# Filler matmuls on TensorE before the first tile, and an earlier copy of tile 0's first half, in a two-layer graph network kernel

## What is computed

```python
h = jnp.maximum(_layernorm(x, axis=-1), 0.0)
x = x + _L0_gnn_ref(h, edge_index, edge_type_2, ...)
h = jnp.maximum(_layernorm(x, axis=-1), 0.0)
x = x + _L1_gnn_ref(h, L1_gnn_W, L1_gnn_a, src, dst)
```

## Time and profile before

| What | us |
|---|---|
| median of 3 runs | 508.41 (508.1 to 508.73) |
| the profiled execution | 509.32 |
| its span, first to last instruction | 507.5 |
| mean granted TensorE clock | 0.998 |

### The profile page before, as it was taken

The page is one execution under the profiler, slowest core; times in us unless marked ns, Lnnn a source line. Parts: engine busy times, 40 slices in busy tenths (PEclk is TensorE's granted clock), DMA queues, the critical chain, the costliest instruction groups (busy, mean ns, idle before and its releaser), DMA issues.

```text
span 507.5 us, 7735 instructions
## 1 busy us (share of the span) xinstructions
PE 491.8 (97%) x2953; PEld 424.1 (84%) x2953; DVE 372.1 (73%) x636; ACT 227.5 (45%) x383; POOL 79.5 (16%) x81
## 2 busy tenths in 40 slices
PE   2999999999999999999999999999999999999996
PEld 2989998989989999898888888888887878777785
DVE  4845886599999999998955555556598877777634
ACT  5765543424866666669722223334133323323211
POOL 1181323200000000002000000000083333322400
PEclk9999999999999999999999999999999999999999
DMA  8972254413013335237921111000032322222211
GB/s 256 232 241 88 81 170 142 128 37 95 22 42 94 102 95 159 82 120 260 329 71 42 40 44 50 29 1 0 1 81 83 93 90 65 77 82 81 82 43 45
DMA packets 22186, 49.15 MB, mean 97 GB/s; under 512 B 4798, under 2 KB 10709, under 8 KB 22018
## 3 DMA queue, kind: packets, MB, share of 16 engines
q1 hardware_dynamic: 20879, 44.66, 29.3%
q0 software_dynamic: 1264, 3.93, 2.2%
HBM read 33.05 MB, written 16.85 MB: 98 GB/s over the span
## 4 chain that ended last, share of the span: by engine, by line
PE 90%; DVE 5%; ACT 3%; DMA 1%; issue 1%; SPq 0%; DVEq 0%; ACTq 0%
PE ps L1359 11%; PE ps L1628 9%; PE ps L1630 9%; PE ps L1629 9%; PE ps L1525 8%; PE ps L1610 7%; PE ps L1611 7%; PE ps L1609 7%; PE ps L1428 4%; PE ps L1447 2%; PE ps L1581 2%; PE ps L1595 2%; PE ps L1583 2%; PE ps L1582 2%; PE ps L1403 1%; PE ps L1406 1%
## 5 line engine op out<-in xcount | busy, mean ns | idle before, releaser
L1628 PE MATMUL ps<-h_hi,att_hi 125*125 125x512 f32 (+1 forms) x190 | 73.5, 387 | 0.0
L1629 PE MATMUL ps<-h_lo,att_hi 125*125 125x512 f32 (+1 forms) x190 | 72.6, 382 | 0.0
L1630 PE MATMUL ps<-h_hi,att_lo 125*125 125x512 f32 (+1 forms) x190 | 72.6, 382 | 0.0
L1609 PE MATMUL ps<-wg,gT_hi 128*125 128x512 f32 x160 | 63.7, 398 | 0.0
L1610 PE MATMUL ps<-wg,gT_hi 128*125 128x512 f32 x160 | 63.1, 394 | 0.0
L1611 PE MATMUL ps<-wg,gT_lo 128*125 128x512 f32 x160 | 63.0, 394 | 0.0
L1525 PE MATMUL ps<-msg_hi,adj_hi 125*125 125x288 f32 x180 | 50.3, 304 | 0.0
L1525 PE MATMUL ps<-msg_lo,adj_hi 125*125 125x286 f32 x180 | 45.9, 295 | 0.0
L708 ACT ACTIVATE em<-ps,rinv 125x512 f32<-125x512 f32 (+1 forms) x21 | 14.0, 669 | 63.1 <-DVE hp L1225 63.1
L1630 PEld LDWEIGHTS ps<-h_hi,att_lo 125*125 125x125 f32 x190 | 35.3, 186 | 8.0
L1628 PEld LDWEIGHTS ps<-h_hi,att_hi 125*125 125x125 f32 x190 | 35.2, 185 | 7.9
(11 more groups left out here) (218 smaller groups left out, 1085.8 us busy)
## 6 DMA issues: line engine op xcount, KB each, us to landing
xt<-in_x SPq DMA_DIRECT2D x10, 448.0 KB
xh_scratch<-xt SPq DMA_DIRECT2D x10, 448.0 KB
xt<-xh_scratch SPq DMA_DIRECT2D x10, 448.0 KB
x_scratch<-xt SPq DMA_DIRECT2D x10, 448.0 KB
x1t<-x_scratch SPq DMA_DIRECT2D x10, 448.0 KB
xr<-x_scratch SPq DMA_DIRECT2D x10, 448.0 KB
out_x<-xr SPq DMA_DIRECT2D x19, 224.0 KB
wg_raw<-in_L_gnn_W POOLq DMA_DIRECT2D x7, 512.0 KB, 7.5
```

The lines of the kernel that those rows point to most:

```text
L1609: M.matmul(to, hi, wg[k][:, 0, cut], start=n == 0, stop=False)
L1628: M.matmul(to, hi[:, s, :], h_hi[:, s, cut], start=s == 0, stop=False)
L1629: M.matmul(to, hi[:, s, :], h_lo[:, s, cut], start=False, stop=False)
L1630: return M.matmul(to, lo[:, s, :], h_hi[:, s, cut], start=False, stop=s == TILES - 1)
```

## The change

Four things. VectorE, after its increments and before its first wait, fills the second half of `junk` with ones and signals `filled`. TensorE, after its own increments, waits for `filled`, multiplies that half with itself ten times (125 rows, 125 columns of weights, 512 columns moved, bf16, into bank 7), then waits for the layer-norm weights as before and transposes them, and multiplies six times more. ScalarE's `first_transposed` and VectorE's `first_low_parts` are each cut in two calls: the first half is done after `norm(0)` on ScalarE, ahead of `deviation(1)`, and after `variance(1)` on VectorE, ahead of `deviation(1)`; the second half keeps its place. The semaphore `msgpad`, which one instruction incremented and none waited for, is gone.

```diff
--- before.py
+++ after.py
@@ -253,7 +253,7 @@
 
         names = """edges_in lnw_in lnw_ps w_split h1_rdy bias_in g_ps wo_split xh_rdy x1_rdy o_ps wg_rdy a_in gT_ps h_dve
             res_rdy zeros consts more_consts sd_rdy ssq_rdy rm_rdy hT_hi_rdy g_act win_out c_used e_rdy yT_hi_rdy
-            g1_rdy gT_hi_rdy h_act att_e att_hi_rdy m_rdy asum_rdy sum_step el_rdy r_ps msgpad var_rdy rstd_rdy hT_ps wraw_hi rms_rdy
+            g1_rdy gT_hi_rdy h_act att_e att_hi_rdy m_rdy asum_rdy sum_step el_rdy r_ps filled var_rdy rstd_rdy hT_ps wraw_hi rms_rdy
             table_rdy x_used hot_used s_ps c_ps wo_hi_rdy yT_ps rs2_rdy sd2_rdy wg_hi_rdy rstd2_rdy h_ps
             al_ps al_rdy att_v att_p p_ps rinv_rdy bn_rdy rs_rdy hT_lo_rdy g_dve win_lo deg_rdy inv_rdy
             z1_rdy zz_rdy y_rdy yT_lo_rdy bn2_rdy mv2_rdy gT_lo_rdy att_u att_lo_rdy den_rdy rr_rdy dchain
@@ -541,10 +541,10 @@
                     last = A.copy(hT_hi[b][:, 4 * h:4 * h + 4, :], first_tp(t, h))
                 last.then_inc(S["hT_hi_rdy"], 1)
 
-            def first_transposed():
-                for h, (came_in, out) in enumerate((("half_hT", "half_hi"), ("hT_ps", "hT_hi_rdy"))):
-                    act.wait_ge(S[came_in], data(0) if h else 1)
-                    A.copy(hT_hi[0][:, 4 * h:4 * h + 4, :], tp_bank(h)).then_inc(S[out], 1)
+            def first_transposed(h):
+                came_in, out = (("half_hT", "half_hi"), ("hT_ps", "hT_hi_rdy"))[h]
+                act.wait_ge(S[came_in], data(0) if h else 1)
+                A.copy(hT_hi[0][:, 4 * h:4 * h + 4, :], tp_bank(h)).then_inc(S[out], 1)
 
             def split_weights(ks):
                 for k in ks:
@@ -560,14 +560,15 @@
             def pads():
                 A.copy(ident_r[:], ident[:])
                 A.copy(msg_hi[:, :, :, F], ones[:].rearrange("p (t r) -> p t r", r=RELS))
-                A.mul(msg_hi[:, :, :, F + 1], ones[:].rearrange("p (t r) -> p t r", r=RELS), 0.0).then_inc(S["msgpad"], 1)
+                A.mul(msg_hi[:, :, :, F + 1], ones[:].rearrange("p (t r) -> p t r", r=RELS), 0.0)
 
             act.wait_ge(S["lnw_ps"], 2)
             deviation(0, 0)
             norm(0, 0)
+            first_transposed(0)
             deviation(1, 1)
             split_weights(range(0, 1))
-            first_transposed()
+            first_transposed(1)
             norm(1, 1)
             split_weights(range(1, 2))
             transposed(1, 1, 0)
@@ -937,11 +938,11 @@
                                            hT_hi[b][:, 4 * h:4 * h + 4, :].bitcast(F32), ALU.subtract)
                 last.then_inc(S["hT_lo_rdy"], 1)
 
-            def first_low_parts():
-                for h, (came_in, out) in enumerate((("half_hi", "half_lo"), ("hT_hi_rdy", "hT_lo_rdy"))):
-                    dve.wait_ge(S[came_in], data(0) if h else 1)
-                    V.tensor_tensor(hT_lo[0][:, 4 * h:4 * h + 4, :], tp_bank(h), hT_hi[0][:, 4 * h:4 * h + 4, :].bitcast(F32),
-                                    ALU.subtract).then_inc(S[out], 1)
+            def first_low_parts(h):
+                came_in, out = (("half_hi", "half_lo"), ("hT_hi_rdy", "hT_lo_rdy"))[h]
+                dve.wait_ge(S[came_in], data(0) if h else 1)
+                V.tensor_tensor(hT_lo[0][:, 4 * h:4 * h + 4, :], tp_bank(h), hT_hi[0][:, 4 * h:4 * h + 4, :].bitcast(F32),
+                                ALU.subtract).then_inc(S[out], 1)
 
             def mean_square(t):
                 dve.wait_ge(S["rm_rdy"], data(t))
@@ -990,12 +991,14 @@
             def stage1(first, end):
                 pipeline((transposed, 1), (messages, 2), (moments, -1), steps=(first, end))
 
+            V.memset(junk[:, HALF:D], 1.0).then_inc(S["filled"], 1)
             dve.wait_ge(S["consts"], 1)
             moments(0, 0, 0)
             variance(1, 1)
+            first_low_parts(0)
             deviation(1, 1)
             split_weights(range(0, 1))
-            first_low_parts()
+            first_low_parts(1)
             split_weights(range(1, 2))
             low_parts(1, 1)
             split_weights(range(2, KT))
@@ -1348,9 +1351,15 @@
                 pe.sem_inc(S[n], CREDIT)
             pe.sem_inc(S["p_ps"], 2 * CREDIT)
             pe.sem_inc(S["c_ps"], 3 * CREDIT)
+            def kept_busy(times):
+                for _ in range(times):
+                    M.matmul(bank(7, T, HALF), junk[0:T, HALF:HALF + T], junk[0:T, HALF:D], start=True, stop=True)
+            pe.wait_ge(S["filled"], 1)
+            kept_busy(10)
             pe.wait_ge(S["consts"], 1)
             pe.wait_ge(S["lnw_in"], 16)
             M.transpose(ps[:, 6, 0:KT], lnw_rows[:], ident[0:KT, 0:KT]).then_inc(S["lnw_ps"], 1)
+            kept_busy(6)
 
             def split_products(out, pairs):
 
```

## The result

| | before | changed |
|---|---|---|
| median, us | 508.39 (508.09 to 508.79, 6 runs) | 511.38 (510.67 to 512.25, 6 runs) |
| ratio | 1 | 1.0061 (95%: 1.0050 to 1.0071) |
| profiled execution, us | 509.32 | 511.22 |
| its span | 507.5 | 509.4 |

The changed kernel is slower by 3.0 us. The forecast was slower, by 1.3 us, at 509.7 in a range of 507.9 to 512.2. The sign was right, and so was the main step, a late tile 0. The size was less than half of what came: 511.4 lies outside the 508.9 to 510.4 that the forecast gave itself, and inside the whole range only because that makes room for rival A, the clock that does not hold.

What follows compares the result with a forecast made beforehand. TensorE's nearly gapless matmul queue bounds the kernel, so opening losses last. Tile 0 3.1 us late, less about 2.0 from clock and packing, gives +1.1; with 0.2 added to the median's figure, 509.7 us, range 507.9 to 512.2 (own range 508.9 to 510.4).

Steps and rivals of the forecast that it cites:

- rival A: TensorE's clock falls in the gaps behind tile 0 or never rises: slower still, up to 512.1 us; chance 0.24.
- Part 1: Opening: ten cold fillers from 4.7 to 8.96 delay the layer-norm weights' transpose, making tile 0's transposes 3.1 us late.
- Part 2: Six fillers after the weights' transpose, 2.56 us cold or 1.4 hot, fill the wait for tile 0 and cost nothing.
- Part 3: Copying tile 0's first half before tile 1's deviation delays slice 0's weight split and first product; charged 0.4 us.
- The sum: Opening: 3.1 us late, less about 2.0 from higher clock and closer packing, gives +1.1 us; afterwards both queues are the same.
- high clock behind tile 0: TensorE stays at 2.4 GHz behind tile 0: product pairs of 0.39 us, tile 1's transposes 1.02 instead of 1.87.
- halfway price: For a clock falling later in the opening, between the forecast's +1.1 us and the worst case's 512.1: 510.8 us.
- The reference: The profiled execution, 509.32 us, 0.9 above the 508.41 median; 0.2 added to the median's figure for a later clock rise.
- The slack: All TensorE idle time lies before 17.3 us and in the last 5 us, so opening losses reach the end almost whole.
- Rivals B: The clock rises early, so the first fill is short (break-even end 7.86): not slower, 508.0 or 507.1 us; chance 0.15.
- C: VectorE's increments are no brake, the fill runs 1.5 to 5.8, tile 0 is on time: 506.4 us; chance 0.06.

Runs made afterwards that it cites:

- late_no_fill: Changed kernel without filler matmuls, the layer-norm weights' transpose held back by eight GpSimd memsets instead; median 511.55 us, ratio 1.0066 to before.
- fill_two_first: Changed kernel with two fillers instead of ten ahead of the weights' transpose, six after it; median 509.41 us, ratio 1.0025 to before.
- fill_only: Changed kernel with its fill, but both copies in the old order, behind slice 0's split; median 510.26 us, ratio 1.0040 to before.
- early_old_order: Changed kernel with the memset on GpSimd, fills of seven and six, and both copies in the old order; median 508.00 us, ratio 0.9995 to before.
- after_gap: Changed kernel with six more filler matmuls in the gap behind tile 0's transposes; median 511.01 us, ratio 1.0056 to before.
- fill_early_pool: Changed kernel with the memset of ones on GpSimd and a first fill of seven; median 508.92 us, ratio 1.0005 to before.
- before_again: The kernel before, unchanged, traced a second time; one execution, 508.99 us.

## Why the prediction came out as it did

**Part 1 (the first fill): right, and it was the main step.** The increments hold the memset to 4.08 (forecast 3.93), it takes 0.48 (0.65 taken, from a row of another operation), the fill starts at 4.62 (4.7) and ends at about 8.5 (8.96). Over both fills the matmuls last 0.69 us at most and 0.38 at least, and ten cold ones were to take 4.26 and took 3.93: the clock rose towards the end of the first fill. The deviation starts at 9.01 (9.50), tile 0 at 11.03 (11.52). late_no_fill and fill_two_first show that this lateness is a cause and no bystander; so do fill_only and early_old_order, both in the old order, which the late fill sets 2.3 us apart (1.0040 and 0.9995). The one cycle per element of the Trainium skill's page "VectorE: DVE Perf Modes", section "Zero memsets can be issued as uint32 (trn2)", had given an estimate of 0.53 us for the memset, which the 0.48 of the trace nearly bears out.

**Part 2 (the second fill costs nothing): right.** Six fillers in 1.51 us, over at 10.22, TensorE then idle for 0.81.

**Part 3 (the reorder): the direction right, its own price too small.** "I charge the reorder 0.4": alone it costs 1.6 us. I had costed it against a trace in which tile 1 had landed late. Where tile 1 is early, the old order splits slice 0 at once, and the new one waits for tile 0's transposes, which are cold without the fill. With the fill the reorder has a second price, that it often lets the clock fall: 20 of 41 executions with the new order and nothing more behind tile 0 are at 0.996 or less, 3 of 31 with the old. Within the changed kernel the split starts at 12.38, and the aggregation at 11.04 plus 0.44 would have allowed 11.48: 0.9. The sum used the new order's own times, so that mistake did not enter it; it did enter two expectations of the experiments.

**The sum: the step that failed is the high clock behind tile 0, "two pairs of 0.39" and "1.02 hot instead of 1.87".** From the deviation to slice 0's w_hi (13.38 for 13.84) every time came about 0.5 before the forecast, and the product with w_lo starts at 14.58 for 15.0. Then the clock fell, at 14.8, 14.5 and 15.3 in the three traces of the changed kernel. The two pairs and tile 1's transposes took 3.31 us (14.58 to 17.89) where the sum had 1.80, and tile 1's low product started at 20.33 instead of 19.25. Behind it the sum's last sentence, "From there both queues are the same and hot", held: from there to tile 2 it is 14.68 us, and 14.57 before. By the pair changed and after_gap a fall costs 1.3 us.

**Rival A therefore came true in part.** Its halfway price was 510.8. The gap it named is the right one (TensorE idle to 13.52, after fillers in it the clock held), and the reorder is what lengthens it: in the three filled traces with the old order and nothing in the gap the clock held, in the five with the new order it fell four times, and the executions without a trace say the same. The Trainium skill's page "TensorE: Matmul & The Clock Gate", section "Part 4: PE-mode transpose", has transposes not counting as work. By it TensorE rests from the last filler to the first product. That is 3.3 us in the changed kernel (10.22 to 13.52) and 3.9 in fill_early_pool, which fell, but 3.4 in early_old_order (7.36 to 10.76), which did not. The runs neither bear the rule out nor settle what decides.

**The reference was off too.** The sum stood against one profiled execution, and I took only 0.2 of its 0.9 us above the median to be a chance of landing and clock. The 3.0 us between the medians add up like this from the two traces: 2.3 in the opening, less 0.4 from the shorter tail, 0.9 by which the traced execution of before lies above its median, and 0.2 by which that of the changed kernel lies below its own. Of the 2.3 in the opening after_gap shows 1.0 with the clock held (33.70 against 32.71), which is nearly the sum's 1.1, and the fall is the other 1.3. So the sum was good against the trace that it was worked out on, partly by luck: the times up to w_hi were 0.5 early. But after_gap, whose clock held in all six executions, is 2.8 us above before's median where the forecast with a clock that holds had 1.3. So 1.5 us of the miss would stand without any fall. The reference makes 0.7 of them (0.9 less 0.2); the rest lies in how openings and tails differ from one execution to the next, which no pair of traces settles. before_again, whose tile 2 starts 0.9 earlier, shows only that an opening can differ by that much.

**The slack.** TensorE also idles for 1.6 us between 33 and 300 us in the kernel before, where the prediction has none. It changed nothing: the delay of the opening, 2.30 us at tile 2, is 2.27 at the last matmul.

**Rivals B and C fell.** The fill ended at 8.5, not before 7.86; the fill waited for the increments, as the earlier trace rows said.

## What to carry to other kernels

A filler must end before the first small instruction that others wait for, counted at the low clock and from when the engine can really start: look at what its operand's producer does first, even if that is only semaphore increments of 0.09 us each. Keeping TensorE fast in an opening is worth little as long as TensorE waits for the engines beside it (0.5 us at best in the old order here); having it fall back in the middle cost 1.3 to 2 us where it happened. Look at single executions too, for a median between two groups describes neither. Take the reference from several executions before laying a sum of tenths against it. And an instruction moved ahead of another takes over its waits: ask in which executions the one moved ahead is the later of the two.

## What the runs showed that I had not expected

- A fall of the clock in mid-opening, with TensorE not resting for more than 1.4 us at a stretch, transposes counted as work, but busy little behind tile 0 (0.10, 0.48 and 0.57 in three windows of 1 us).
- The 470 us behind tile 2 take the same time to within 0.1 us in all fourteen traces, though the tails behind them differ by 1.4: in the traces the spread is made ahead of tile 2 and in the last 6 us.
- Two groups of executions of one kernel, 2 us apart, told apart by a mean granted clock of 0.997 or more and 0.996 or less (fill_early_pool). In the other kernels that show both kinds, their times overlap.
